# Two graphs routed by one router sum in an attention, expert and batch-norm kernel

## What is computed

```
x = _layernorm(x + L0(x, adj, adj, Wq, Wk, Wv, Wo))
# second layer, on the new x
scores = x.mean(axis=1) @ router_w + router_b
top1 = argmax(scores, axis=-1)                  # one of 4 experts for each graph
support = einsum('bnh,bhk->bnk', x, expert_w[top1])
out = einsum('bnm,bmk->bnk', adj, support)
s, ss = segment_sum(out.sum(1), top1), segment_sum((out * out).sum(1), top1)
cnt = maximum(graphs of the expert * 128, 1)
mean, var = s / cnt, ss / cnt - (s / cnt) ** 2  # for each expert and feature
y = (out - mean[top1]) * rsqrt(var[top1] + 1e-5) * gamma[top1] + beta[top1]
result = _layernorm(x + relu(y))
```

## Time and profile before

| | us |
|---|---|
| median of 3 runs | 2863.39 (2861.16 to 2863.82) |
| the profiled execution | 2862.67 |
| its span, from the first to the last instruction | 2860.9 |
| attention stage, in the span | 0 to 2013 |
| expert stage | 2013 to 2573 |
| norm stage, head | 2573 to 2608 |
| norm stage, loop and end | 2608 to 2861 |

### The profile page before, as it was taken

The page is one execution under the profiler, slowest core; times in us unless marked ns, Lnnn a source line. Parts: engine busy times, 40 slices in busy tenths (PEclk is TensorE's granted clock), DMA queues, the critical chain, the costliest instruction groups (busy, mean ns, idle before and its releaser), DMA issues. The chain is left out here.

```text
span 2860.9 us, 79162 instructions
## 1 busy us (share of the span) xinstructions
PE 2714.6 (95%) x22786; PEld 2264.8 (79%) x22787; DVE 2256.1 (79%) x8801; ACT 1450.0 (51%) x5261; POOL 1276.4 (45%) x1171
## 2 busy tenths in 40 slices
PE   8999999999999999999999999998699999997776
PEld 7888888888888888888888888887577777774232
DVE  6788888888788888878888888888577777766998
ACT  5656556566565565665665655655222222222444
POOL 2343333333333333334333333333366666665786
PEclk9999999999999999999999999999799999997998
DMA  3111111211211111111111111120334344436998
GB/s 142 60 56 51 60 56 49 62 51 52 63 51 52 59 55 54 52 59 56 51 60 56 51 60 53 50 63 24 119 126 130 118 126 127 129 104 216 376 375 323
DMA packets 169425, 277.30 MB, mean 97 GB/s; under 512 B 19378, under 2 KB 52146, under 8 KB 168882
## 3 DMA queue, kind: packets, MB, share of 16 engines
q1 hardware_dynamic: 150962, 243.36, 26.4%
q10 hardware_dynamic: 18432, 33.56, 3.1%
HBM read 184.57 MB, written 92.27 MB: 97 GB/s over the span
## 5 line engine op out<-in xcount | busy, mean ns | idle before, releaser
L512 POOL TENSOR_TENSOR probs<-probs,row_scale 128x512 f32<-128x512 f32 x512 | 532.8, 1041 | 1091.2 <-DVE row_scale L408 1091.0
L316 ACT ACTIVATE probs<-neg_s,neg_max 128x128 f32<-128x128 f32 x2048 | 793.2, 391 | 139.3 <-DVE neg_max L384 139.3
L384 DVE CUSTOM_DVE_ANT_0 neg_s<-att_bank,adj_nat 128x128 f32<-128x128 f32 x2048 | 442.6, 286 | 4.6 <-PE att_bank L197 2.3
L316 ACT ACTIVATION_READ_ACCUMULATOR probs<-neg_s,neg_max 128x1 f32 x2048 | 388.3, 190 | 0.0
L393 DVE TENSOR_REDUCE abs_max<-neg_s 128x4 f32<-128x512 f32 x512 | 349.2, 682 | 0.1
L176 PE MATMUL att_bank<-xt_hi,att_w_hi 128*128 128x256 f32 x2048 | 329.4, 283 | 11.0 <-DVE att_w_lo L366 11.0
L176 PE MATMUL att_bank<-xt_hi,att_w_lo 128*128 128x256 f32 x2048 | 329.8, 283 | 0.0
L176 PE MATMUL att_bank<-xt_lo,att_w_hi 128*128 128x256 f32 x2048 | 329.3, 283 | 0.0
L176 PEld LDWEIGHTS att_bank<-xt_hi,att_w_hi 128*128 128x128 f32 x2048 | 298.8, 191 | 30.5 <-issue 10.6
L344 ACT ACTIVATE probs_t<-att_bank 128x512 f32<-128x512 f32 x256 | 153.2, 599 | 299.0 <-PE att_bank L235 298.9
L176 PEld LDWEIGHTS att_bank<-xt_hi,att_w_lo 128*128 128x128 f32 x2048 | 282.8, 192 | 0.0
(11 more groups left out here) (120 smaller groups left out, 5502.8 us busy)
## 6 DMA issues: line engine op xcount, KB each, us to landing
xt_stage<-in_x_t SPq DMA_DIRECT2D x64, 512.0 KB, 3.6
x_nat<-in_x SPq DMA_DIRECT2D x128, 256.0 KB, 2.6
x_scratch<-x SPq DMA_DIRECT2D x128, 256.0 KB, 2.0
g_x<-x_scratch SPq DMA_DIRECT2D x128, 256.0 KB, 2.8
n_x<-x_scratch SPq DMA_DIRECT2D x128, 256.0 KB, 5.6
out_x<-n_out ACTq DMA_DIRECT2D x128, 256.0 KB, 5.7
y_scratch<-g_out SPq DMA_DIRECT2D x96, 256.0 KB, 2.0
n_y<-y_scratch SPq DMA_DIRECT2D x96, 256.0 KB, 5.1
```

The source lines that it names most:

```text
L316: nc.scalar.activation(probs[:, h * P:(h + 1) * P], neg_s[:, h * P:(h + 1) * P], ACT.Exp, bias=neg_max[:, h:h + 1], scale=-1.0, accum_out= ...
L384: nc.vector.tensor_tensor_reduce(neg_s[:, h * P:(h + 1) * P], bank[r][:, c * P:(c + 1) * P], adj_nat[:, s], -2.0, BIG, ALU.add, ALU.min, n ...
L512: nc.gpsimd.tensor_tensor(part, part, by, ALU.mult).then_inc(probs_done, 1)
```

## The change

The attention stage stays as it is.

**Expert stage.** The scores of two graphs, t + 1 and t + 2, are made by one matmul in odd steps, between the first and the second pass of `out_product`; its weights are 128 columns of ones, not one. `route` handles both graphs at once and writes two numbers; PE waits for them only in even steps, right ahead of the register load, and takes the odd step's number behind the even step's `out_product`. `products` reads the node sums from PSUM and comes ahead of `y_lo`; `y_hi` waits for it. The copies of `ps_o` go from DVE to ACT, for a kept graph straight into `kept`; the square reads `ps_o`, and PE waits for the square before it writes that bank again.

```
+            def router_scores(pair):
+                pe.wait_ge(part_done, 2 * pair + 2)
+                pe.wait_ge(expert_done, pair + 1)
...
+                    if m == C:
+                        after_one_pass()
...
             def body(t, s, i, last, ends):
-                pe.wait_ge(expert_done, t + 2)
...
+                    pe.wait_ge(expert_done, 2 * i + s // 2 + 2)
+                    e = load_expert(t)
...
+                    if s % 2 and exists(t, last, 2):
+                        router_scores(2 * i + s // 2 + 1)
...
             def y_high(t, s):
-                act.wait_ge(y_ps, t + 1)
+                act.wait_ge(products_done, t + 1)
...
+                nc.scalar.activation(dst, ps_o[s % 2][:, :], ACT.Copy).then_inc(out_done, 1)
                 act.wait_ge(sqsum_done, t + 1)
-                nc.scalar.activation(sq[:, s % 2], out[:, s], ACT.Square).then_inc(sq_done, 1)
+                nc.scalar.activation(sq[:, s % 2], ps_o[s % 2][:, :], ACT.Square).then_inc(sq_done, 1)
...
+                nc.vector.tensor_copy(expert_row[:, bass.ds(at, 2)], best_at[:, :, 0]).then_inc(expert_done, 1)
```

```
-    RING = 8
+    RING = 16
...
-                    sp.wait_ge(z_done, t + 1 + RING)
-                    load(t + RING, s)
+                    if not is_kept(s):
+                        sp.wait_ge(sum_ps, t + 1)
+                        load_y(t + RING, s)
+                    sp.wait_ge(stored[s], i * 16 + 16)
+                    load_x1(t + RING, s)
...
+                    mm = pe.matmul(ps_sums[:, :], sum_into[:, 2 * E - 1 - n:4 * E - 1 - n], acc[:, e, :], start=n == 0, stop=n == 2 * E - 1)
...
+                    for k in range(UNROLL):
+                        nc.vector.bn_aggr(mean_var[:, k], stats[:, k]).then_inc(mv_done, 1)
```

More of the change, by code:

```diff
@@ L565, in expert_phase @@
         y_hi, y_lo = sb("y_hi", [P, UNROLL, D], F32R), sb("y_lo", [P, UNROLL, D], F32R)
[L566 to L571, removed]
+        products = sb("products", [P, 2, E, C])
+        part_score = sb("part_score", [P, 2, E])
+        scores = sb("scores", [1, 2, 8])
+        best = sb("best", [1, 2, 8])
+        best_at = sb("best_at", [1, 2, 8], U32)
         out = sb("g_out", [P, UNROLL, D])
@@ L750, in route @@
                 dve.sem_inc(route_go, 1)
-                nc.vector.max(best[:, :], scores[:, :]).then_inc(best_done, 1)
-                dve.wait_ge(best_done, t + 1)
+                for g in range(2):
+                    nc.vector.max(best[:, g], scores[:, g]).then_inc(best_done, 1)
+                dve.wait_ge(best_done, 2 * pair + 2)
                 dve.sem_inc(route_go, 1)
-                nc.vector.max_index(best_at[:, :], best[:, :], scores[:, :]).then_inc(best_at_done, 1)
-                dve.wait_ge(best_at_done, t + 1)
@@ L756, in route @@
[L756 removed]
+                for g in range(2):
+                    nc.vector.max_index(best_at[:, g], best[:, g], scores[:, g]).then_inc(best_at_done, 1)
+                dve.wait_ge(best_at_done, 2 * pair + 2)
+                nc.vector.tensor_copy(expert_row[:, bass.ds(at, 2)], best_at[:, :, 0]).then_inc(expert_done, 1)
             dve.sem_inc(expert_done, 1)
             dve.sem_inc(y_lo_done, 2)
[L760 removed]
@@ L911, in _ @@
         def _(pe):
+            pe.wait_ge(into_done, 2)
             for w, acc in enumerate((out_sum, out_sq)):
                 for e in range(E):
-                    for c in range(C):
-                        mm = pe.matmul(ps_cols[:, w, e * C + c:e * C + c + 1], acc[:, e, c * P:(c + 1) * P],
-                                       ones[:, 0:1], start=True, stop=True)
-            mm.then_inc(cols_ps, 1)
-            pe.wait_ge(step, 3)
-            pe.matmul(ps_count[:, :], ones[0:1, :], graphs[:, :], start=True, stop=True).then_inc(count_ps, 1)
@@ L922, in _ @@
-            for w in range(2):
-                pe.wait_ge(diag_done, w + 1)
-                for e in range(E):
-                    n = w * E + e
-                    if n >= 2:
-                        pe.wait_ge(rows_done, n - 1)
-                    for c in range(C):
-                        mm = pe.matmul(ps_rows[n % 2][:, c * P:(c + 1) * P], ones[:, :],
-                                       diag[:, w, e * C + c, :], start=True, stop=True)
-                    mm.then_inc(rows_ps, 1)
-            pe.wait_ge(picks, 3)
@@ L934, in _ @@
-            pe.wait_ge(rows_done, 2 * E)
+                    n = w * E + e
+                    mm = pe.matmul(ps_sums[:, :], sum_into[:, 2 * E - 1 - n:4 * E - 1 - n], acc[:, e, :], start=n == 0, stop=n == 2 * E - 1)
+            mm.then_inc(sums_ps, 1)
+            pe.wait_ge(step, 3)
+            pe.matmul(ps_count, ones[0:1, :], graphs[:, :], start=True, stop=True).then_inc(count_ps, 1)
+            pe.wait_ge(sums_done, 1)
+            for c in range(C):
+                mm = pe.transpose(ps_cols[:, c, :], sums_sb[:, c * P:(c + 1) * P], ident[0:2 * E, 0:2 * E])
```

278 lines of the change are left out of this document (152 added, 126 removed).

## The result

The changed kernel takes 2797.2 us (median of 4 runs, 2795.3 to 2798.7) against 2863.2 us: a ratio of 0.977, with a 95% interval of 0.9753 to 0.9787. That is 66 us less where 57 were forecast, inside the stated range, in its faster half. The span of the profiled execution went from 2860.9 to 2794.7 us.

What follows compares the result with a forecast made beforehand. Expert stage taken as bound by TensorE's work and waits, norm loop by transfers or something at their pace, norm head by a chain. 36 + 2 + 19 = 57 us off 2863.4 gave 2806 us, range 2790 to 2822.

Steps and rivals of the forecast that it cites:

- Array: Expert stage, TensorE: matmuls of a pair of graphs need 7.42 us plus 0.25 for the scores, 7.67 if nothing waits.
- Chain: Expert stage: odd ps_y through products, y_lo, route and number load to even out_product, 4.96 us; 7.86 us a pair.
- The round's gap: Expert stage, TensorE: the 0.77 us once per round of eight goes away, with eight long matmuls queued behind the scores.
- The gain of a pair: Expert stage: a pair of graphs falls from 8.37 to 7.8 us, 36 us over 63 pairs, between 1 and 44.
- The head of the expert stage: Start of expert stage: ps_y of graph 1 no longer stands behind the scores of graph 0, about 2 us gained.
- What moved to ScalarE: Expert stage: ps_o copy and kept tile add 0.6 us a graph, ScalarE busy some 216 of 514 us; covered.
- Norm head: Start of norm stage: first n_y 21.0 us after the start, 8 us earlier; first n_rstd 11.7 us earlier.
- Norm loop: Norm stage's loop: four graphs take 7.55 us instead of 7.67, transfers full at 382 GB/s; 3.7 us gained.
- The route stays the bound: Rival, expert stage: chain at 8.35 us a pair, TensorE waits before every even out_product; 2841 us, chance 0.22 shared with no-effect.
- A two-element copy takes the port: Rival, expert stage: the 1x2 number copy waits for GpSimd's sum, 9.1 us a pair; 2888 us, chance 0.05.
- The transfers hold the norm loop: Rival, norm loop: today's beat or above as reloads wait for stores, 19 becomes 6; 2819 us, inside the forecast's 0.62.
- The pairing changes nothing: Rival, expert stage: TensorE waits as long as before at another place; 2842 us, within the shared chance of 0.22.

Runs made afterwards that it cites:

- e9: Changed kernel with the route ahead of y_lo on VectorE and the two expert numbers written by two one-element copies: 2786.2 us, ratio 0.9728.
- e4: Changed kernel with the odd step's route ahead of y_lo on VectorE instead of behind it: 2789.5 us, ratio 0.9742.
- e5: Kernel before, with only products reading node sums from PSUM ahead of y_lo, y_hi after it, one route per graph: 2838.3 us, ratio 0.9917.
- e6: Kernel before, with the norm loop's seven small operations replaced by four bn_aggr and two tensor_scalar, ring of eight kept: 2848.1 us, ratio 0.9952.
- e7: Changed kernel with the norm loop's seven small operations back in place of bn_aggr, ring of 16 kept: 2808.5 us, ratio 0.9819.
- e3: Changed kernel with node sums first copied to SBUF and products reading them there, ahead of y_lo: 2871.1 us, ratio 1.003.

## Why the prediction was right, point by point

- **Array.** 7.67 us a pair if nothing waits: with the even step's wait gone (e9) it is 7.58. The scores cost 0.14 us and 0.08 in the pass behind them, 0.22 for the 0.25 that I took.
- **Chain.** The sum was 4.96 us to the even `ps_o` and 7.86 to the next odd `ps_y`; the timeline has 2214.23 - 2209.35 = 4.88 and 7.76. Of its pieces, `ps_y` to the start of the route is 2.56 us (2.71 forecast), the route 1.33 (1.35), and from the end of its copy to the even `ps_o` 0.99 (0.9, the term that no row showed; the register load itself is 0.30 of it). That array and chain nearly meet was the right picture, and e4 and e9 show the chain as the one that ends last.
- **The round's gap.** It went as forecast, but the eight matmuls queued behind the scores are not needed for it: e5 loses it without them.
- **The gain of a pair.** Between the same `ps_y` of successive pairs, from 2060 to 2500 us, the kernel before takes 8.39 us, not the 8.37 of the count of rows, and the changed one 7.76, not 7.8: 0.63 us instead of 0.57, so some 39 us instead of 36.
- **The head of the expert stage.** About 2 us were forecast there, from the scores of graph 0. The loop's first `ps_y` moved by 0.17, since TensorE waits at that place for the experts' weights to be cut, in the kernel before

```profile
2033.34 2.08 PE L651 MATMUL ps_y<-adj_t,g_x 128*128 128x129 f32 x8 [5.99 <-DVE exp_w_lo L765]
```

as in the changed one:

```profile
2033.17 2.08 PE L652 MATMUL ps_y<-adj_t,g_x 128*128 128x129 f32 x8 [8.10 <-DVE exp_w_lo L781]
```

The 2 us that did not come and the 3 that the pairs gave beyond the sum nearly cancel: that the stage's 38.9 us stand so close to the 38 is in part luck.

- **What moved to ScalarE** is covered, as forecast: it is busy for 197 of 464 us, and `ps_o` follows `ps_y` after 0.81 us in every odd step, so TensorE does not wait for the square.
- **Norm head.** 21.0 us to the first `n_y` were worked out, 1.3 of them for GpSimd's fills, which now lie ahead of the first matmul; from that matmul on 22.2 came, for 19.7. The sums over the partitions took 8.7 us (2533.91 to 2542.6) for the 5.9, and the price of a pass was the error: I took 0.23 us from `ps_o`, whose operands are fp32r, but these are fp32, and one pass of 512 columns follows the other after 0.43 us where the granted clock is 1.00 (2.4 GHz, 2539 to 2542 us) and after 0.85 where it is 0.50 (1.2 GHz, 2536 to 2538; TensorE had stood idle for 4.00 us ahead of these sums). The earlier trace rows had the better row, two fp32 passes of `ps_z` in 1.12 us. The 32 short matmuls took 5.3 us (2549.71 to 2555.05, at a granted clock of 0.50, behind idle stretches of 4.80 and 0.77 us) where I had 4.2 for 28. Other steps came out shorter, so the head missed by less than its terms did: the first `n_rstd` gained 10.4 us of the 11.7.
- **Norm loop: the mis-sized term.** I took 7.55 us a beat because 382 GB/s over 30 us, with a DMA share of 1.03, looked like full transfers, and left the 7.1 us that GpSimd's chain allowed for the end of the range. e6 and e7 show that 382 was the demand of a loop held by VectorE's small operations. The beat of 7.06 is worth 16.7 us where I gave the loop and its preload 7.3. The ring's preload, which I had at up to 9.6 us, gives 1 to 4 together with the writing in place.
- **A rule weighed.** Against the 358 GB/s of the Trainium skill, DMA: Bandwidth & Descriptors, section Specifications, I had set the measured 382; 406 GB/s over 120 us stand further off still. The row gives the figure as half of 716 GB/s, the share of one of two cores, and this kernel runs on one, so it need not have bound here; but 382 was no bound either.
- **The rivals.** *The route stays the bound*: it does bind, but by 0.16 us a pair (0.97 us from the even `ps_y` to `ps_o` at the median, 0.81 in e9) where this rival has 0.7. *A two-element copy takes the port*: the mechanism is there, as e4 and e9 show; the changed kernel escapes it because the copy comes just when `out_sq` ends. I had reckoned with 0.3 us between them, and there is nothing to spare. *The transfers hold the norm loop*: not at the old beat; they come in 0.1 us a beat behind GpSimd's own limit. *The pairing changes nothing*: what it brings, with the copies moved to ScalarE, is 16 of the expert stage's 39 us, and with the wrong operand for `products` it is a loss (e3).

## What to carry to other kernels

Before a queue is rearranged around a late small operation, compare its shortest and its median duration: where they differ by a factor of five, ask what runs beside it on GpSimd, and give it an operand from PSUM or a single element at a time; here that alone brought 23 us. Limits that lie within a few per cent of each other have to be costed together, since the gain from the first ends where the second begins. Read the room that transfers have from their GB/s in short slices and in several kernels, not from a mean or from a share that stands near one.

## What the hardware showed that I had not expected

- The DMA share reads 0.99 at 329 GB/s and 1.05 at 354 as at 405, so it is no measure of how full the transfers are.
- A copy of two elements in one partition waits for a running GpSimd sum (425 ns at the median), copies of one element don't (142 ns each). In the changed kernel 56 of the 64 copies begin in the last 0.04 us of the sum and the other 8 outside one, and none of them waits: 155 to 158 ns.
- From the finished copy of an expert number to the first matmul with it TensorE takes 0.99 us at the median of the even steps, 0.30 of it the register load itself, more than VectorE's `y_lo` of 512 elements (0.69 us).
